# Pieces in neighbouring slots, one read per job, and half of the exponentials ahead of the carry copy

## The chip, the cores and the metric

The kernel runs on one core of one Trainium2 chip. The metric is the device time of one execution in microseconds; smaller is better. A core has five engines that each run their own instructions in order and wait for one another by semaphores: TensorE (PE in the profile, its weight loads PEld), VectorE (DVE), ScalarE (ACT), GpSimd (POOL) and SyncE (SP), which here issues the DMAs.

## The reference, cut to what matters

One block of a bidirectional selective state-space model for 16 sequences of 256 steps with 256 channels. Both directions run over all 16 sequences.

```
h, gate = adaln(x, c, ...)                    # normalise, scale, shift
def ssm(h, in_w, xproj_w, dt_bias, A_log, D, out_w):
    xs, z = split(h @ in_w)                   # 512 channels each
    xs = silu(xs)
    proj = xs @ xproj_w
    dt = softplus(proj[..., :512] + dt_bias)
    B, C = proj[..., 512:576], proj[..., 576:]
    A = -exp(A_log)                           # 512 channels x 64 states
    for t in steps:
        state = state * exp(dt_t * A) + (dt_t * xs_t) * B_t
        y_t = sum over states of state * C_t
    return (y + xs * D) * silu(z) @ out_w
x = x + gate * (ssm_forward(h) + flip(ssm_backward(flip(h))))
return x + gate2 * (silu(h2 @ w1) * (h2 @ w2) @ w3)
```

Before `proj`, the inputs of the two directions are prepared by matmuls. The sum over time with 512 x 64 states for each sequence and direction is the bulk of the work.

## The kernel before

There are two phases. `output_phase` does the last projections and is untouched. `main_phase` does all the rest in 16 **passes** (`PASSES`), one for each pair of sequences and direction. A pass has 128 **slots** (`JP`): eight chunks of 32 time steps, each with 16 slots. Slot j is one scan instruction of VectorE on 128 partitions (2 sequences x 64 states) by 1024 columns (32 channels x 32 steps), which holds two halves, h = 0 and 1, of 16 channels.

What a slot asks for, with the line numbers of the profile:

- **Inject** (TensorE, L1044, eight records a slot): spreads dt x xs x B into the PSUM tile `u`. `u` has two places, taken by j % 2, so the inject of slot j waits until scan j - 2 has ended.
- **Exponent** (TensorE, L1057, four records): for the slot j + 2, dt x A of half 0 and of half 1, each into one PSUM bank of 512 columns. They stand behind the inject of slot j. There are three banks (`NDT`, named `b_ex0` to `b_ex2`); `share_banks` hands them out in a fixed order, and what gets a bank waits until its last content has been read.
- **Decay** (ScalarE, `decay`, L802 and L803): for the slot j + 2, for each half, the exponential of the first column (`b_first`, only where there is a carry) and of the 31 others (`b_dA`). It frees the bank.
- **Carry** (GpSimd L578, L583, then ScalarE `put_carry`, L821): from the second chunk on, that is in slots 16 to 127, the state left by the chunk before is multiplied by the first decay, added to the first input, and copied by ScalarE over column 0 of `u`, once the inject of the same slot is there. The scan waits for it.
- **Scan** (VectorE, L894).
- **Readout** (TensorE, `add_up`, L1076): of the scans of eight slots before, in the odd slots, 16 records each; ScalarE reads the result every eighth slot (L814).

Beside this, in the slots of pass p the inputs of pass p + 1 are made in 31 **jobs**, laid into slots by the tables `XZ_SLOT`, `DT_SLOT`, `BC_SLOT`, `UT_SLOT`, `BT_SLOT`, `TURN_SLOT`. TensorE runs a piece of a job behind the slot's own work (`unit`): in an XZ job (L947) two matmuls of 128 x 256, in a DT or BC job (L955) four in two pieces, in a UT job or a turn job transposes. A job takes one of the three banks until ScalarE has read it: a DT job for three slots before the change. ScalarE's `unit` reads each job at the end of a slot (L658 and L661 for XZ, L677 and L678 for DT), works on it in SBUF (L665, L684 to L694), and changes its function table three times a pass (at L726, L741, L760). GpSimd multiplies and adds (L472 to L497). Passes 0, 2, ..., 12 also make the normalised input of the next pair of sequences: two turn jobs, of which each is read by ScalarE in two slots (`modulate`, L636). In the last pass there are no jobs.

ScalarE's order in slot j is: the carry copy of slot j, the decay of slot j + 2 (both halves), the read of the readout, the side work of `unit`. TensorE's order is: inject j, the exponents of j + 2, readout, job piece.

## Time and profile before

| what | us |
|---|---|
| median of 3 runs | 5272.7 (5270.68 to 5274.25) |
| the profiled execution | 5272.6 |
| its span, first to last instruction | 5270.9 |
| first scan starts, last scan ends (in the span) | 106.9, 4816.9 |
| VectorE busy in the span | 4721.3 |
| TensorE busy in the span | 4869.9 |
| ScalarE busy in the span | 3384.6 |
| idle time of VectorE ahead of a scan | 184.5 |

The profile is of one execution. Its times count from the first instruction. In a timeline each row is a run of like instructions that follow closely: its start, its length, engine, line, operation, output and inputs, their count, and in brackets the idle time of the engine before it with what ended it. The records of an engine overlap a little: a scan is recorded as 2.26 us long, and three that follow each other closely take less than three times that.

### The profile page before, as it was taken

Reading aid. Unit: us, or ns where it says so; the run is one execution under the profiler, and the core shown is the slowest. Engines: PE = TensorE matmul, PEld = TensorE weight load, DVE = VectorE, ACT = ScalarE, POOL = GpSimd, SP = SyncE. Lnnn points to the kernel's source line nnn. Section 1 sums busy time; section 2 is a strip of 40 time slices with the busy share of each in tenths; the row PEclk is TensorE's granted clock in tenths of the full one; section 3 lists DMA queues with packets and bytes.
Section 4 is the critical chain, followed back from the end, with each engine's and each line's share of the span. In section 5 each row is a group of like instructions: output and inputs, shape, how many; then the busy total and the mean of one; then the engine's idle time right before and its main releaser. Section 6 shows DMA issues by size and latency. Waiting matters only on the chain. (4 is left out here: it accounts for less than half of the span.)

```text
span 5270.9 us, 130492 instructions
## 1 busy us (share of the span) xinstructions
PE 4869.9 (92%) x44784; PEld 2658.3 (50%) x44784; DVE 4721.3 (90%) x2419; ACT 3384.6 (64%) x11498; POOL 3754.7 (71%) x6613
## 2 busy tenths in 40 slices
PE   6999999999999999999999999999999999776898
PEld 4555555555555555555555555555555555443444
DVE  2999999999999999999999999999999999996443
ACT  4767767676766766676766767676676767663112
POOL 4787878777787878777787878687887878674211
PEclk8999999999999999999999999999999999998999
DMA  3121211112121211112121211111121211113442
GB/s 107 39 65 45 65 38 54 56 39 62 43 61 44 66 41 50 56 40 62 43 61 43 67 40 52 55 45 56 43 61 43 64 40 46 31 29 111 145 153 68
DMA packets 433144, 306.75 MB, mean 58 GB/s; under 512 B 215920, under 2 KB 336240, under 8 KB 432496
## 3 DMA queue, kind: packets, MB, share of 16 engines
q1 hardware_dynamic: 428272, 294.39, 18.7%
q8 instruction: 349, 5.72, 0.4%
q10 hardware_dynamic: 4224, 4.19, 0.2%
q14 instruction: 299, 2.45, 0.1%
HBM read 187.27 MB, written 111.15 MB: 57 GB/s over the span
## 5 line engine op out<-in xcount | busy, mean ns | idle before, releaser
L894 DVE TENSOR_TENSOR_SCAN b_hs<-b_dA,b_u 128x1024 f32<-128x1024 f32 x2048 | 4536.0, 2270 | 184.5 <-ACT b_u L821 155.5
L1057 PE MATMUL b_ex<-b_dd,b_aw 32*128 32x512 f32 x8192 | 2751.5, 641 | 17.6 <-POOL b_dd L542 15.6
L1044 PE MATMUL b_u<-b_ud,b_bw 32*128 32x256 f32 x16384 | 2320.1, 400 | 276.9 <-DVE b_hs L894 255.9
L803 ACT ACTIVATE b_dA<-b_ex 128x496 f32<-128x496 f32 x4096 | 2303.5, 593 | 166.0 <-PE b_ex L1057 127.5
L1044 PEld LDWEIGHTS b_u<-b_ud,b_bw 32*128 32x128 f32 x16384 | 1417.5, 184 | 1122.7 <-issue 558.1
L821 ACT ACTIVATE b_u<-b_hin 128x32 f32<-128x32 f32 x1792 | 368.8, 206 | 1236.8 <-PE b_u L1044 1045.4
L542 POOL TENSOR_TENSOR b_dd<-b_dr,b_mask 128x512 f32<-128x512 f32 x1024 | 1074.9, 1050 | 51.5 <-DVE b_hs L894 39.8
L1076 PE MATMUL b_y<-b_hs,b_cw 128*32 128x256 f32 x16384 | 1104.8, 385 | 1.7 <-DVE b_hs L894 1.7
L551 POOL TENSOR_TENSOR b_ud<-b_ur,b_mask 128x512 f32<-128x512 f32 x1024 | 1085.6, 1060 | 0.0
L1057 PEld LDWEIGHTS b_ex<-b_dd,b_aw 32*128 32x128 f32 x8192 | 865.4, 183 | 62.0 <-ACT b_dA L803 35.7
L1076 PEld LDWEIGHTS b_y<-b_hs,b_cw 128*32 128x32 f32 x16384 | 426.9, 108 | 846.2 <-issue 663.3
L578 POOL TENSOR_TENSOR b_hm<-b_first,b_hs 128x32 f32<-128x32 f32 x1792 | 487.6, 272 | 443.5 <-ACT b_first L802 421.9
L802 ACT ACTIVATE b_first<-b_ex 128x16 f32<-128x16 f32 x3584 | 652.4, 182 | 56.4 <-PE b_ex L1057 33.2
L583 POOL TENSOR_TENSOR b_hin<-b_hm,b_u 128x32 f32<-128x32 f32 x1792 | 452.9, 253 | 140.4
L955 PE MATMUL b_ex<-b_xs,b_wxp 128*128 128x256 f32 x1256 | 353.4, 405 | 3.9 <-ACT b_ey L678 2.8
L1211 POOL TENSOR_TENSOR c_gs<-c_gs,c_sz 128x512 f32<-128x512 f32 x64 | 79.0, 1279 | 299.8 <-DVE c_gs L1417 299.8
L947 PE MATMUL b_ex<-b_hT,b_win 128*128 128x256 f32 x1004 | 285.9, 408 | 3.1 <-ACT b_hT L636 3.1
L955 PEld LDWEIGHTS b_ex<-b_xs,b_wxp 128*128 128x128 f32 x1256 | 214.5, 189 | 138.8 <-issue 118.6
L947 PEld LDWEIGHTS b_ex<-b_hT,b_win 128*128 128x128 f32 x1004 | 173.2, 191 | 117.5 <-issue 76.9
L477 POOL TENSOR_TENSOR b_ey<-b_wy,b_ey 128x512 f32<-128x512 f32 x64 | 83.4, 1304 | 202.5 <-ACT b_wy L694 202.5
L472 POOL TENSOR_TENSOR b_xs<-b_xs,b_th 128x512 f32<-128x512 f32 x64 | 81.4, 1273 | 193.2 <-ACT b_th L665 193.2
L472 POOL TENSOR_TENSOR b_sd<-b_sd,b_th 128x512 f32<-128x512 f32 x64 | 81.3, 1270 | 85.4 <-ACT b_th L665 85.4
(104 smaller groups left out, 2351.0 us busy)
## 6 DMA issues: line engine op xcount, KB each, us to landing
b_u<-scratch_ut SPq DMA_DIRECT2D x256, 128.0 KB, 2.9
scratch_y<-b_ysb SPq DMA_DIRECT2D x128, 256.0 KB, 2.1
scratch_xs<-b_xs SPq DMA_DIRECT2D x64, 256.0 KB, 2.5
scratch_sz<-b_sd SPq DMA_DIRECT2D x64, 256.0 KB, 2.2
scratch_dt<-b_sd SPq DMA_DIRECT2D x64, 256.0 KB, 2.1
scratch_ut<-b_uT SPq DMA_DIRECT2D x64, 256.0 KB, 2.6
b_ur<-scratch_ut SPq DMA_DIRECT2D x1024, 16.0 KB
b_dr<-scratch_dt SPq DMA_DIRECT2D x1024, 16.0 KB, 1.7
```

The lines of the kernel that those rows point to most:

```text
L542: nc.gpsimd.tensor_tensor(dd[:, (p * PAIRS + i) % NDD, :, :], dr[:, c % 2, v:v + 1, :].broadcast_to((P, TT, TC)), mask[:, :].unsqueeze(2). ...
L551: nc.gpsimd.tensor_tensor(ud[:, i % NPR, :, :, :], ur[:, c % 2, :, v * TT:(v + 1) * TT].unsqueeze(3).broadcast_to(shape), mask[:, :].unsqu ...
L578: nc.gpsimd.tensor_tensor(hm[:, j % NM, :, :].rearrange("p h d -> p (h d)"), e0[:, j % NM, :, :].rearrange("p h d -> p (h d)"), hs[:, v, : ...
L583: nc.gpsimd.tensor_tensor(hin[:, j % NM, :, :], hm[:, j % NM, :, :], u0[:, c % 2, 2 * kp:2 * kp + 2, v, :], ALU.add).then_inc(hin_made, 1)
L802: nc.scalar.activation(e0[:, j % NM, h, :], src[:, :, 0], ACT.Exp).then_inc(e0_done, 1)
L803: nc.scalar.activation(dA[:, j % NDA, h, :, 1:TC], src[:, :, 1:TC], ACT.Exp).then_inc(exp_done, 1)
L894: nc.vector.tensor_tensor_scan(hs[:, v, :, :, kp].rearrange("p d t -> p (d t)"), dA[:, j % NDA, :, :, :].rearrange("p h d t -> p (h d t)") ...
L947: last = nc.tensor.matmul(job_bank(n)[:, 0:SEQ], win[:, k, i * P:(i + 1) * P], hT[:, q % DIRS, k, b * SEQ:(b + 1) * SEQ], start=(k == 0), ...
L955: ins = nc.tensor.matmul(job_bank(n)[:, 0:SEQ], wxp[:, k, cols], xs[:, k, b * SEQ:(b + 1) * SEQ], start=(k == 0), stop=(k == JB - 1))
L1044: ins = nc.tensor.matmul(dst[:, :, tb, :], bw[row(r), c % 2, tb, :], ud[row(r), j // 2 % NPR, tb, :, :], start=(tb == 0), stop=(tb == NTB ...
L1057: nc.tensor.matmul(e[bank_of[what]][:, :], aw[row(r), p % DIRS, v, :, :].rearrange("p b s -> p (b s)"), dd[row(r), (p * PAIRS + j // 2) % ...
L1076: ins = nc.tensor.matmul(y[q * QR:(q + 1) * QR, cols], cw[:, n, q, g * QR:(g + 1) * QR], hs[:, f * (SPN // 2):(f + 1) * (SPN // 2), :, q * ...
```

## The change

Five things change in `main_phase`.

1. **ScalarE's slot.** `decay` is split by halves. The order in slot j is now: decay of slot j + 2, half 0; carry copy of slot j; a **read** of a job, if there is one; decay of slot j + 2, half 1; read of the readout; a step of the **work** on what was read. `unit` is split into two generators for it, `readers` and `works`.
2. **One read per job.** An XZ job is only copied out of its bank (`take_xz`); the tanh is then taken of both sequences at once from SBUF (`bend`, new). A DT job is read once with its bias into `pre`; Abs and Relu are taken later from SBUF at 512 columns. A semaphore `relued` is added, for which GpSimd's `sum_dt` waits, and `bent_up` ahead of `plus_one`.
3. **Slots.** The two pieces of a pair stand in neighbouring slots (0, 1), (4, 5) and so on, and the two pieces of a DT or BC job too, so that it holds its bank for two slots in place of three. All pieces now start at j % 4 = 0 or 1.
4. **Readouts** stand in the slots with j % 4 = 2 or 3, still two groups of eight records in each of four slots out of eight.
5. **Banks.** `share_banks` reckons with a bank of half 1 as free 0.5 slots after that of half 0 (0.25 before) and with one of a job 0.1 after its last slot. GpSimd's steps are moved by a few slots.

```diff
-        XZ_SLOT = ((0, 2), (4, 6), (8, 10), (12, 14), (16, 18), (86, 88), (98, 100), (104, 106))
-        DT_SLOT, DT_SPAN = (22, 38, 54, 70), 3
-        BC_SLOT, BC_SPAN = (32, 48), 3
-        UT_SLOT, UT_SPAN = (64, 80, 82, 96), (2, 2, 1, 1)
-        BT_SLOT = 66
+        XZ_SLOT = ((0, 1), (4, 5), (8, 9), (12, 13), (16, 17), (84, 85), (92, 93), (100, 101))
+        DT_SLOT, DT_SPAN = (20, 36, 52, 68), 2
+        BC_SLOT, BC_SPAN = (28, 44), 2
+        UT_SLOT = (60, 76, 80, 96)
+        BT_SLOT = 61
...
-                        give(("e", 2 * (slot + 2) + h), slot + 0.9 + 0.25 * h)
+                        give(("e", 2 * (slot + 2) + h), slot + 0.9 + 0.5 * h)
...
-                        give(("job", n), slot + slots + 0.2)
+                        give(("job", n), slot + slots + 0.1)
...
-                    nc.scalar.activation(dst[:, cols], job_bank(n)[:, 0:SEQ], ACT.Copy, scale=0.5)
-                    if m >= 2:
-                        act.wait_ge(silu_made, m - 1)
-                    nc.scalar.activation(th[:, i % 2, cols], job_bank(n)[:, 0:SEQ], ACT.Tanh, scale=0.5).then_inc(freed, 1)
+                    nc.scalar.activation(dst[:, b * SEQ:(b + 1) * SEQ], job_bank(n)[:, 0:SEQ], ACT.Copy, scale=0.5
+                                         ).then_inc(freed, 1)
+
+                def bend(q, i):
+                    m = q * SILUS + i
+                    src = xs[:, i, :] if i < JB else sd[:, i - JB, :]
+                    act.wait_ge(freed, first_job(q) + XZ_JOB[i] + CB)
+                    if m >= 2:
+                        act.wait_ge(silu_made, m - 1)
+                    nc.scalar.activation(th[:, i % 2, :], src, ACT.Tanh).then_inc(bent_up, 1)
...
-                    nc.scalar.activation(pre[:, m % 2, cols], job_bank(n)[:, 0:SEQ], ACT.Relu, bias=bias)
-                    nc.scalar.activation(ey[:, cols], job_bank(n)[:, 0:SEQ], ACT.Abs, bias=bias).then_inc(freed, 1)
+                    nc.scalar.activation(pre[:, m % 2, b * SEQ:(b + 1) * SEQ], job_bank(n)[:, 0:SEQ], ACT.Identity,
+                                         bias=dtb[:, q % DIRS, j:j + 1]).then_inc(freed, 1)
...
+                    nc.scalar.activation(ey[:, :], pre[:, m % 2, :], ACT.Abs).then_inc(bent, 1)
...
+                    nc.scalar.activation(pre[:, m % 2, :], pre[:, m % 2, :], ACT.Relu).then_inc(relued, 1)
...
+                        then = (p, j + 2) if j + 2 < JP else None if last else (p + 1, j + 2 - JP)
+                        if then:
+                            decay(*then, 0)
                         if j >= STEPS:
                             put_carry(p, j)
-                        if j + 2 < JP:
-                            decay(p, j + 2)
-                        elif not last:
-                            decay(p + 1, j + 2 - JP)
+                        next(reads, None)
+                        if then:
+                            decay(*then, 1)
                         if j % HALF == 0 and half >= 2:
                             read_y(half - 2)
-                        next(side, None)
+                        next(work, None)
...
-                    if k % 2 and half:
-                        add_up(half - 1, k % HALF - 1)
-                        add_up(half - 1, k % HALF)
+                    if k % 4 >= 2 and half:
+                        n = k % HALF // 4 * 2 + k % 4 - 2
+                        add_up(half - 1, 2 * n)
+                        add_up(half - 1, 2 * n + 1)
```

ScalarE before, slots 17 and 18 of the first pass (L821 is the carry copy, L802 and L803 the decay): the carry copy, then both halves, in each slot.

```order
L821 ACTIVATE b_u<-b_hin 128x32 [waits b_u_done3,b_u_done2,b_hin_made]
L802 ACTIVATE b_first<-b_ex2 128x16 [waits b_e_done0,b_hin_made,b_scanned]
L803 ACTIVATE b_dA<-b_ex2 128x16x31
L802 ACTIVATE b_first<-b_ex0 128x16 [waits b_e_done1]
L803 ACTIVATE b_dA<-b_ex0 128x16x31
L821 ACTIVATE b_u<-b_hin 128x32 [waits b_u_done1,b_u_done0,b_hin_made]
L802 ACTIVATE b_first<-b_ex1 128x16 [waits b_e_done2,b_hin_made,b_scanned]
L803 ACTIVATE b_dA<-b_ex1 128x16x31
L802 ACTIVATE b_first<-b_ex2 128x16 [waits b_e_done3]
L803 ACTIVATE b_dA<-b_ex2 128x16x31
```

The same engine after the change, slot 17 and the start of slot 18 (L835 and L836 are the decay, L854 the carry copy, L663 the read of an XZ job):

```order
L835 ACTIVATE b_first<-b_ex2 128x16 [waits b_e_done0,b_hin_made,b_scanned]
L836 ACTIVATE b_dA<-b_ex2 128x16x31
L854 ACTIVATE b_u<-b_hin 128x32 [waits b_u_done3,b_u_done2,b_hin_made]
L663 ACTIVATE b_sd<-b_ex0 128x256 [waits b_dt_stored0,b_full]
L835 ACTIVATE b_first<-b_ex1 128x16 [waits b_e_done1]
L836 ACTIVATE b_dA<-b_ex1 128x16x31
L835 ACTIVATE b_first<-b_ex2 128x16 [waits b_e_done2,b_hin_made,b_scanned]
L836 ACTIVATE b_dA<-b_ex2 128x16x31
L854 ACTIVATE b_u<-b_hin 128x32 [waits b_u_done1,b_u_done0,b_hin_made]
L835 ACTIVATE b_first<-b_ex0 128x16 [waits b_e_done3]
```

The carry copy moved behind the first half, and the read of the job stands between the carry copy and the second half.

TensorE before, slots 0 to 2 of the first pass, from the first job piece on (L947); `b_ex0` to `b_ex2` are the three banks:

```order
L947 MATMUL b_ex0<-b_hT,b_win 128x256 [waits b_exp_done,b_freed,b_win_loaded]
L947 MATMUL b_ex0<-b_hT,b_win 128x256
L1044 MATMUL b_u<-b_ud,b_bw 128x16x16 [waits b_scanned]
L1044 MATMUL b_u<-b_ud,b_bw 128x16x16 x3
L1057 MATMUL b_ex1<-b_dd,b_aw 128x512 [waits b_exp_done]
L1057 MATMUL b_ex2<-b_dd,b_aw 128x512 [waits b_exp_done]
L1044 MATMUL b_u<-b_ud,b_bw 128x16x16 [waits b_scanned,b_ud_made,b_dd_made]
L1044 MATMUL b_u<-b_ud,b_bw 128x16x16 x3
L1057 MATMUL b_ex0<-b_dd,b_aw 128x512 [waits b_freed]
L1057 MATMUL b_ex1<-b_dd,b_aw 128x512 [waits b_exp_done]
L947 MATMUL b_ex2<-b_hT,b_win 128x256 [waits b_exp_done]
```

TensorE after, the same place (L984 job piece, L1083 inject, L1096 exponent):

```order
L984 MATMUL b_ex0<-b_hT,b_win 128x256 [waits b_exp_done,b_freed,b_win_loaded]
L984 MATMUL b_ex0<-b_hT,b_win 128x256
L1083 MATMUL b_u<-b_ud,b_bw 128x16x16 [waits b_scanned]
L1083 MATMUL b_u<-b_ud,b_bw 128x16x16 x3
L1096 MATMUL b_ex1<-b_dd,b_aw 128x512 [waits b_exp_done]
L1096 MATMUL b_ex0<-b_dd,b_aw 128x512 [waits b_freed]
L984 MATMUL b_ex2<-b_hT,b_win 128x256 [waits b_exp_done]
L984 MATMUL b_ex2<-b_hT,b_win 128x256
L1083 MATMUL b_u<-b_ud,b_bw 128x16x16 [waits b_scanned,b_ud_made,b_dd_made]
L1083 MATMUL b_u<-b_ud,b_bw 128x16x16 x3
L1096 MATMUL b_ex1<-b_dd,b_aw 128x512 [waits b_exp_done]
L1096 MATMUL b_ex2<-b_dd,b_aw 128x512 [waits b_freed]
L1083 MATMUL b_u<-b_ud,b_bw 128x16x16 [waits b_scanned]
```

The piece of slot 2 moved to slot 1. An exponent that waits for the read of a job (`b_freed`) was that of half 0, two slots after the piece; it is now that of half 1, one slot after the piece.

ScalarE before, slot 113 of the first pass, where the second half of a turn job is read:

```order
L821 ACTIVATE b_u<-b_hin 128x32 [waits b_u_done3,b_u_done2,b_hin_made]
L802 ACTIVATE b_first<-b_ex2 128x16 [waits b_e_done0,b_hin_made,b_scanned]
L803 ACTIVATE b_dA<-b_ex2 128x16x31
L802 ACTIVATE b_first<-b_ex0 128x16 [waits b_e_done1]
L803 ACTIVATE b_dA<-b_ex0 128x16x31
L636 ACTIVATE b_hT<-b_ex1,mod 128x256 x2
```

and after:

```order
L835 ACTIVATE b_first<-b_ex2 128x16 [waits b_e_done0,b_hin_made,b_scanned]
L836 ACTIVATE b_dA<-b_ex2 128x16x31
L854 ACTIVATE b_u<-b_hin 128x32 [waits b_u_done3,b_u_done2,b_hin_made]
L643 ACTIVATE b_hT<-b_ex0,mod 128x256 x2
L835 ACTIVATE b_first<-b_ex0 128x16 [waits b_e_done1]
L836 ACTIVATE b_dA<-b_ex0 128x16x31
```

The reading of the turned input (two instructions, L636 before and L643 after) stood behind both halves of the decay; it now stands between them.

## Rows read from the trace of the kernel before

**Rows 1.** The page: busy time by engine; and the costliest group (columns: busy, mean ns | idle, releaser).

```profile
PE 4869.9 (92%) x44784; PEld 2658.3 (50%) x44784; DVE 4721.3 (90%) x2419; ACT 3384.6 (64%) x11498; POOL 3754.7 (71%) x6613
...
L894 DVE TENSOR_TENSOR_SCAN b_hs<-b_dA,b_u 128x1024 f32<-128x1024 f32 x2048 | 4536.0, 2270 | 184.5 <-ACT b_u L821 155.5
```

**Rows 2.** The scans (L894) in passes 2, 3 and 15: window, length, busy time, clock, DMA.

```profile
698.18:994.90 296.72, 284.17 (x130) 1.00 0.17 50
994.90:1289.18 294.28, 283.58 (x130) 1.00 0.18 53
...
4538.00:4816.90 278.90, 278.88 (x129) 0.99 0.09 25
```

**Rows 3.** The same of pass 3: slots 0-15, 20-35 and 84-103.

```profile
994.90:1030.98 36.08, 35.48 (x17) 1.00 0.17 49
...
1040.42:1078.30 37.88, 35.60 (x17) 1.00 0.16 47
...
1190.17:1235.66 45.49, 43.98 (x21) 1.00 0.29 86
```

**Rows 4.** Timeline (start, us, engine) of slots 40 to 42 of the last pass.

```profile
4622.97 6.62 DVE L894 TENSOR_TENSOR_SCAN b_hs<-b_dA,b_u 128x1024 f32<-128x1024 f32 x3
...
4623.20 0.48 PE L1044 MATMUL b_u<-b_ud,b_bw 32*128 32x256 f32 x2
...
4624.46 0.20 ACT L821 ACTIVATE b_u<-b_hin 128x32 f32<-128x32 f32 x1 [0.92 <-PE b_u L1044]
...
4625.28 0.48 PE L1044 MATMUL b_u<-b_ud,b_bw 32*128 32x256 f32 x2 [0.93 <-DVE b_hs L894]
...
4626.57 0.20 ACT L821 ACTIVATE b_u<-b_hin 128x32 f32<-128x32 f32 x1 [0.45 <-PE b_u L1044]
...
4627.56 0.48 PE L1044 MATMUL b_u<-b_ud,b_bw 32*128 32x256 f32 x2
```

**Rows 5.** Timeline of slot 14 of the last pass, where no carry is copied.

```profile
4566.58 0.48 PE L1044 MATMUL b_u<-b_ud,b_bw 32*128 32x256 f32 x2
...
4567.88 0.18 ACT L802 ACTIVATE b_first<-b_ex 128x16 f32<-128x16 f32 x1 [1.20 <-PE b_ex L1057]
...
4568.42 0.19 ACT L802 ACTIVATE b_first<-b_ex 128x16 f32<-128x16 f32 x1
```

**Rows 6.** Timeline of slots 18 and 19 of pass 2: a piece, then a readout.

```profile
737.37 0.48 PE L1044 MATMUL b_u<-b_ud,b_bw 32*128 32x256 f32 x2
...
738.45 1.13 PE L947 MATMUL b_ex<-b_hT,b_win 128*128 128x256 f32 x4
738.65 0.20 ACT L821 ACTIVATE b_u<-b_hin 128x32 f32<-128x32 f32 x1 [1.24 <-PE b_u L1044]
...
738.98 4.46 DVE L894 TENSOR_TENSOR_SCAN b_hs<-b_dA,b_u 128x1024 f32<-128x1024 f32 x2 [0.25 <-ACT b_u L821]
...
739.38 0.60 ACT L803 ACTIVATE b_dA<-b_ex 128x496 f32<-128x496 f32 x1
...
739.51 0.48 PE L1044 MATMUL b_u<-b_ud,b_bw 32*128 32x256 f32 x2
...
740.03 0.69 PE L1057 MATMUL b_ex<-b_dd,b_aw 32*128 32x512 f32 x1
...
742.09 0.48 PE L1044 MATMUL b_u<-b_ud,b_bw 32*128 32x256 f32 x2
```

**Rows 7.** Timeline of slot 6 of pass 2: a piece and its read.

```profile
711.17 1.13 PE L947 MATMUL b_ex<-b_hT,b_win 128*128 128x256 f32 x4
...
712.34 0.39 ACT L658 ACTIVATE b_xs<-b_ex 128x256 f32<-128x256 f32 x1
```

**Rows 8.** Timeline of slots 28 and 29 of pass 2: a table load and the scan behind.

```profile
763.78 1.28 ACT L741 ACT_TABLE_LOAD   x1
...
765.07 0.20 ACT L821 ACTIVATE b_u<-b_hin 128x32 f32<-128x32 f32 x1
```

**Rows 9.** Timeline of slot 113 of pass 2: the turned input is read.

```profile
960.94 1.11 ACT L636 ACTIVATE b_hT<-b_ex,mod 128x256 f32<-128x256 f32 x2
```

More of the change, by code:

```diff
@@ L178, in main_phase @@
         bent = sem("b_bent")
+        relued = sem("b_relued")
         logged = sem("b_logged")
@@ L765, in unit, with works @@
+                    if q % DIRS == 1 and q + 1 < PASSES:
+                        for k in range(MB):
+                            yield from modulate(q // DIRS + 1, k)
+                            yield from wait_steps(2)
+                def works(q):
+                    nc.scalar.preload_act_table_set("exp_and_others")
+                    yield from wait_steps(2)
+                    for i in range(JB + 1):
+                        bend(q, i)
                         yield
                         plus_one(q, i)
[L767 to L774 removed]
@@ L780, in _ @@
+                    nc.scalar.preload_act_table_set("exp_and_others")
+                    yield from wait_steps(4)
+                    for i in range(JB + 1, SILUS):
+                        bend(q, i)
+                        yield
+                        plus_one(q, i)
+                        yield from wait_steps(7)
                 act.wait_ge(made, 6)
@@ L786, in _ @@
                         pass
-                for _ in unit(0):
-                    pass
+                reads, work = readers(0), works(0)
+                for _ in range(JP):
+                    next(reads, None)
+                    next(work, None)
                 act.wait_ge(a_loaded, 16 * RT * DIRS * CB)
```

175 lines of the change are left out of this document (92 added, 83 removed).

## The prediction

> **What bounds the kernel now.** I read the busy times first. VectorE spends 4536.0 us of the 5270.9 us span in 2048 scans; its 184.5 us of idle time ahead of them is mostly (155.5 us) ended by ScalarE's carry copy [rows 1]. TensorE is busy about as long, so it is the second suspect. Then the passes: the last pass, which carries no jobs, takes 278.9 us, which is 128 scans at 2.178 us from start to start and no wait (three in 6.62 us, less 2.26 for the last [rows 4]); a pass with jobs takes 294.3 us, and 296.7 us where turn jobs are added [rows 2]. So jobs cost 15.4 and 17.8 us a pass, some 245 us in all, and that is the most that a better arrangement can bring. Inside a pass, 16 slots without a wait would take 34.85 us; rows 3 show 36.1 for slots 0 to 15, 37.9 for slots 20 to 35, and 45.5 where 20 slots need 43.6.
>
> Next, what a slot may take without holding the scan, from the job-free pass [rows 4]. Scans start at 4622.97, 4625.15 and 4627.33 and end 2.26 later. The inject starts 0.05 or 0.15 after the end of the scan that frees its place of u (4625.23 to 4625.28, 4627.41 to 4627.56). The carry copy starts 1.26 or 1.29 after the inject (4623.20 to 4624.46, 4625.28 to 4626.57). A scan that waits starts 0.33 after the start of the carry copy (738.65 to 738.98 [rows 6]). In rows 4 it starts 0.69 and 0.76 after it, so the slack is 0.36 us in the slot whose inject came 0.15 late and 0.43 in the other. The whole chain (scan ends, inject, carry, scan after next) has less than half a microsecond to spare even with no jobs.
>
> **Half of the decay ahead of the carry copy.** TensorE still runs inject, then exponents. The exponent of half 0 is ready for ScalarE no earlier than the inject is: where no carry stands before it and ScalarE idled for 1.20 us, its first exponential starts 1.30 after the inject (4566.58 to 4567.88), and the next half starts 0.54 later (4568.42) [rows 5]. So the carry copy can start 1.84 to 1.88 after the inject in place of 1.26 to 1.29, later by 0.58. Of that the slack covers 0.36 or 0.43. What is left, 0.22 or 0.15, sits in a loop that spans two scans, hence 0.11 or 0.075 a slot, 0.095 on average. A slot with a carry takes at least 2.178 + 0.095 = 2.27 us, four of them 9.1. This holds in all 112 carry slots of every pass. In the last pass nothing else changes: 112 x 0.095 = +10.6 us. What hides it where a job holds TensorE is nothing: there the inject itself is late.
>
> The Trainium skill (ScalarE: Activation LUTs, What ACT_TABLE_LOAD costs) gives an ACTIVATE with immediates 186 ns + 0.833 ns a column and lets neighbours overlap by about 93 ns. An estimate from that page is 0.61 us for a half (16 and 496 columns), not the 0.54 of rows 5; the floor would rise by a further 0.035 a slot, about 60 us over 1792 slots.
>
> **Pieces of jobs.** A piece in slot 18 starts 1.08 after the inject, and the next inject comes 2.14 after the last (737.37, 738.45, 739.51) [rows 6]. In the slot behind it, an exponent finds its bank still held: it starts 0.52 after the inject (740.03) in place of 0.03, since ScalarE's half 1 ran until 739.98 (739.38 + 0.60), and that slot takes 2.58 (to 742.09). A readout slot without such a hold takes 2.09. So before, a piece and the slot behind it take 4.72 us.
>
> After, that exponent waits for the read of the job. The read starts 0.04 after the piece ends (711.17 + 1.13 = 712.30 to 712.34) and takes 0.39 to 0.41 [rows 7]: inject + 1.08 + 1.13 + 0.04 + 0.40 = 2.65, and 0.05 to TensorE. The exponent then starts 2.70 - 2.14 = 0.56 after its inject, 0.53 late. Getting ScalarE out of the bank earlier by dropping the tanh brings nothing, as the read now stands between carry copy and half 1 and waits for the piece. With two pieces in neighbouring slots, two exponents are held: 2.14 + (2.14 + 0.53) + (2.09 + 0.53) + 2.09 = 9.5 us for four slots, against 2 x 4.72 = 9.44. DT pieces: half 1 holds the slot of the second piece by 0.54, the longer read (0.52) the next by 0.65, in all 9.65; BC 9.55. The number of holds is thus the same; they are only bunched.
>
> By stretch of slots, after: 0 to 15 have no carry and four XZ pairs, 3 x 9.5 and 9.8 for the first (a table load of 1.28 us [rows 8] stands behind slot 0's half 1, and delays the next slot's halves), 38.4 in all against 36.1 [rows 3], where half 1 ends earlier than in a carry slot and the hold was half as long. 16 to 19: 9.5. 20 to 51: two of 9.65 + 9.65 + 9.55 + 9.1 = 75.9. 52 to 83: two of 9.65 + 9.65 + 9.2 + 9.1 = 75.2. 84 to 103: three XZ pairs, one UT, one empty, 46.9 against 45.5 [rows 3]. 104 to 127: 6 x 9.1 = 54.6. The sum is 300.5 us.
>
> **Turn jobs.** The second half of a turned input is read behind the carry copy, for 1.11 us [rows 9], and the exponent of half 1 waits for it and the decay of half 1 for that. Inject + 1.33 + 0.55 + 0.14 + 1.11 + 0.05 = 3.18; its second record 0.53 later and 0.52 more to the next inject make a slot of 4.23 in place of 2.27. Twice a pass: +3.9, 304.4 us.
>
> **What is hidden or small.** Table loads: before, one stood behind two reads and the next carry copy had to follow it directly (763.78 + 1.28, then 765.07 [rows 8]); that wait of about a microsecond, and a like one later in the pass, go away, since in slots 22 and 82 the load now stands in a slot without a read. This is in the stretches above, as their sums have no term for it. Relu and Abs from SBUF cost ScalarE one more 512-column step a DT job; works stand behind half 1, where in rows 6 ScalarE waits for TensorE, and the read that they replace was as long. The wait on `relued` is met many slots ahead of `sum_dt`; behind it on GpSimd stand the next carries, which would be held if it were not. GpSimd (71% busy) gets the first decay of half 1 up to 0.6 us later in read slots, and has two slots before the carry is due. No DMA is added or resized. In the prologue the order of the same reads moves; I bound it by 3 us either way and take 0.
>
> The same page says that a table load costs 1.28 us and a drain of 1.38 more; rows 8 show the carry copy 0.01 us behind the load, so the trace doesn't bear the drain out. By the page, two loads a pass would hold a carry by about 1.5 us more each, some 45 us.
>
> **The sum.** Eight passes without turn jobs: 300.5 - 294.3 = +6.2 each, 50. Seven with: 304.4 - 296.7 = +7.7 each, 54. The last: +10.6. Together +114 us. The profiled execution took 5272.6 us (span 5270.9, 1.7 around it), 0.1 from the median of three runs, so the sum is 5387 us.
>
> **Rivals.** (a) The holds vanish. If the read freed the bank before the next exponent needs it (a piece that is ready sooner than rows 6 and 7 say), every group with pieces falls to 9.1, slots 0 to 15 stay at 36.1: 28 x 9.1 + 36.1 = 290.9 a pass, 3.4 less than now, with turn jobs 294.8, 1.9 less, and the last pass +10.6: 8 x 3.4 + 7 x 1.9 - 10.6 = 30 us faster, 5243. Against it speaks that TensorE must end the piece first. (b) The half is free. If the exponent of half 0 came ahead of the inject, or the carry copy were mostly late for GpSimd's sake, the half would run in idle time; up to the 155.5 us of waits go, and I price it at two thirds, 5170. Rows 5 speak against the first, and rows 4, where the carry copy is released by TensorE, against the second. (c) Worse than forecast: reads, a step of the logarithm and a late half 1 stack up in one ScalarE slot (slots 29, 45, 61), or GpSimd gets its first decay too late, and a carry is another microsecond late four times a pass: 15 x 4 = +60, 5447. (d) Nothing comes of it: gains and losses cancel within 10 us, as when the holds shrink by half. That the change doesn't do what it says is excluded by the order of the instructions.
>
> **How the numbers follow.** Forecast 0.70, (a) 0.08, (b) 0.06, (c) 0.12, (d) 0.04. A measurement can tell 0.2% (10 us) from no change. Faster is (a) and (b), 0.14; same is (d), 0.04; slower is the forecast and (c), 0.82. The range takes the forecast with the 0.05 or 0.15 of the inject (0.05 a slot in two scans, 0.025 x 1792 = 45 us), holds of 0.3 to 0.65, and (c): 5300 to 5470.
>
> **What would show it.** The scans of the last pass 2.27 us apart on average, from slot 16 on, and about 289 us for that pass. The carry copy 1.84 to 1.88 after the inject. In job slots, the exponent of half 1 about 0.56 after the inject, released by the read, in two slots of four. Slots 0 to 15 of a pass near 38.4. Idle time of VectorE behind the carry copy well above the 155.5 us of rows 1, and in most of the 1792 slots that have one. Waits for table loads gone. I am wrong if the last pass stays near 279 (rows 5 don't carry over), or if passes with jobs fall below 294.

## The result, and the profile after

The change makes the kernel slower by 5.9%: 5582.6 us (5579.09 to 5584.69) against 5272.1, ratio 1.0588 [1.057, 1.0606]. The forecast was 5387 us with a range of 5300 to 5470. The direction was right, the size was not: of the 310 us lost, 114 were foreseen. All times here and below are medians without two far slower executions, one of the kernel before (11121 us) and one of the kernel before with bunched readouts (8971 us).

Page of the changed kernel, in the columns of [rows 1]: VectorE's scans are L931 now, the carry copy L854, the first exponential L835, and L1096 is the exponent on TensorE.

```profile
PE 4847.9 (87%) x44784; PEld 2679.9 (48%) x44784; DVE 4802.2 (86%) x2419; ACT 3441.0 (62%) x11370; POOL 3757.5 (67%) x6613
...
L931 DVE TENSOR_TENSOR_SCAN b_hs<-b_dA,b_u 128x1024 f32<-128x1024 f32 x2048 | 4616.7, 2279 | 414.5 <-ACT b_u L854 325.4
...
L835 ACT ACTIVATE b_first<-b_ex 128x16 f32<-128x16 f32 x3584 | 664.3, 185 | 1364.9 <-PE b_ex L1096 1230.6
```

Two things stand out against [rows 1]. The idle time ahead of the scans went from 184.5 to 414.5 us, and the busy time of the scans grew too, by 81 us: the records of scans that follow closely overlap, those behind a wait do not (and are 2.29 us long, not 2.26). The scans and their idle time sum to 5031 us, 311 more than before, so the whole loss sits in the scan phase.

The cores view adds what no row of the page says loudly. Mean granted TensorE clock of the changed kernel, and of the kernel before:

```profile
core 0: 5580.1 us, clock 0.949
```

```profile
core 0: 5270.9 us, clock 0.989
```

The scans (L931) of the changed kernel in the last pass, in pass 5 (no turn jobs) and in pass 4 (turn jobs): window, length, busy time, clock, DMA. These answer to [rows 2].

```profile
4799.38:5124.38 325.00, 287.99 (x129) 0.86 0.08 22
1672.26:1979.48 307.22, 288.65 (x129) 0.98 0.17 50
1355.07:1672.26 317.19, 288.37 (x129) 0.96 0.16 47
```

The forecast had 289.5, 300.5 and 304.4 for them. The pass that carries no jobs, and should be the simplest to price, is the one that it missed by most, and it has the lowest clock. A mean of 0.86 over 325 us, with levels of 1 and one half, is 91 us at the lower level (1.2 GHz, the upper being 2.4), in 21 stretches. In the last pass of the kernel before it is 3 us. (These lengths, and those of low clock below, are counted in the trace's record of the granted clock; the rounded means of the rows give them within 3 us.)

Timeline of slots 44 to 46 of the last pass (ScalarE's carry copy, TensorE's inject L1083 and readout L1115, the scans):

```profile
4905.72 0.48 PE L1083 MATMUL b_u<-b_ud,b_bw 32*128 32x256 f32 x2 [0.36 <-DVE b_hs L931]
...
4907.56 0.21 ACT L854 ACTIVATE b_u<-b_hin 128x32 f32<-128x32 f32 x1
...
4907.81 0.48 PE L1083 MATMUL b_u<-b_ud,b_bw 32*128 32x256 f32 x2 [0.93 <-DVE b_hs L931]
...
4909.68 0.21 ACT L854 ACTIVATE b_u<-b_hin 128x32 f32<-128x32 f32 x1
...
4910.34 0.79 PE L1083 MATMUL b_u<-b_ud,b_bw 32*128 32x256 f32 x2 [1.37 <-DVE b_hs L931]
...
4912.37 1.73 PE L1115 MATMUL b_y<-b_hs,b_cw 128*32 128x256 f32 x16
...
4913.11 0.21 ACT L854 ACTIVATE b_u<-b_hin 128x32 f32<-128x32 f32 x1
...
4913.45 2.29 DVE L931 TENSOR_TENSOR_SCAN b_hs<-b_dA,b_u 128x1024 f32<-128x1024 f32 x1 [1.09 <-ACT b_u L854]
```

Slots 44 and 45 are as forecast: the carry copy starts 1.84 and 1.87 after its inject. These two slots hold neither piece nor readout. Behind them TensorE is at half speed: the first two records of the inject take 0.79 in place of 0.48, the carry copy of slot 46 starts 2.77 after its inject, and the scan idles 1.09. TensorE's row for slots 40 to 43 and for 44 and on (columns: us, PE busy, clock, DMA):

```profile
4896.49:4905.72 9.23, 6.57 (x80) 1.00 0.08 29
4905.72:4914.91 9.19, 6.89 (x64) 0.81 0.14 30
```

At full clock four slots without jobs take 9.23 us. The clock is down behind slots 45, 49, 53 and 57, and four slots then take 10.3 to 11.7; behind slots 37 and 41 it stays up. All 21 stretches of low clock in this pass begin at the end of the second of two such empty slots, or within 0.6 us behind it.

### The profile page after: what moved, and what is told of

Its sections match the earlier page's. It is cut to its first block and busy times, and to the rows that moved or that the text cites. A ratio compares the mean times of both kernels' runs of the same rounds, so it can differ in the third digit from the quotient of the medians.

```text
span 5580.1 us, 130554 instructions
## 1 busy us (share of the span) xinstructions
PE 4847.9 (87%) x44784; PEld 2679.9 (48%) x44784; DVE 4802.2 (86%) x2419; ACT 3441.0 (62%) x11370; POOL 3757.5 (67%) x6613
## 5 line engine op out<-in xcount | busy, mean ns | idle before, releaser
L931 DVE TENSOR_TENSOR_SCAN b_hs<-b_dA,b_u 128x1024 f32<-128x1024 f32 x2048 | 4616.7, 2279 | 414.5 <-ACT b_u L854 325.4
L1083 PE MATMUL b_u<-b_ud,b_bw 32*128 32x256 f32 x16384 | 2449.4, 414 | 584.1 <-DVE b_hs L931 542.1
L1096 PE MATMUL b_ex<-b_dd,b_aw 32*128 32x512 f32 x8192 | 2688.3, 669 | 44.2 <-ACT b_hT L643 27.8
L836 ACT ACTIVATE b_dA<-b_ex 128x496 f32<-128x496 f32 x4096 | 2399.2, 589 | 188.3 <-PE b_ex L1096 177.2
L1083 PEld LDWEIGHTS b_u<-b_ud,b_bw 32*128 32x128 f32 x16384 | 1503.5, 191 | 1481.9 <-issue 862.8
L835 ACT ACTIVATE b_first<-b_ex 128x16 f32<-128x16 f32 x3584 | 664.3, 185 | 1364.9 <-PE b_ex L1096 1230.6
L1115 PE MATMUL b_y<-b_hs,b_cw 128*32 128x256 f32 x16384 | 1185.2, 408 | 1.0 <-DVE b_hs L931 1.0
L1096 PEld LDWEIGHTS b_ex<-b_dd,b_aw 32*128 32x128 f32 x8192 | 798.1, 190 | 52.2 <-ACT b_hT L643 33.6
L1115 PEld LDWEIGHTS b_y<-b_hs,b_cw 128*32 128x32 f32 x16384 | 446.0, 113 | 734.7 <-issue 573.1
L854 ACT ACTIVATE b_u<-b_hin 128x32 f32<-128x32 f32 x1792 | 375.4, 209 | 5.5 <-PE b_u L1083 5.5
L984 PE MATMUL b_ex<-b_hT,b_win 128*128 128x256 f32 x1004 | 285.1, 408 | 3.1 <-ACT b_hT L643 3.1
L984 PEld LDWEIGHTS b_ex<-b_hT,b_win 128*128 128x128 f32 x1004 | 172.9, 191 | 143.2 <-ACT b_dA L836 77.9
L577 POOL TENSOR_TENSOR b_u<-b_u,b_b 128x256 f32<-128x256 f32 x224 | 137.4, 613 | 0.0
L847 ACT ACTIVATE b_ysb<-b_y 128x128 f32<-128x128 f32 x512 | 120.2, 306 | 8.0 <-PE b_y L1115 8.0
```

Of the source, the lines that this page charges most:

```text
L835: nc.scalar.activation(e0[:, j % NM, h, :], src[:, :, 0], ACT.Exp).then_inc(e0_done, 1)
L836: nc.scalar.activation(dA[:, j % NDA, h, :, 1:TC], src[:, :, 1:TC], ACT.Exp).then_inc(exp_done, 1)
L931: nc.vector.tensor_tensor_scan(hs[:, v, :, :, kp].rearrange("p d t -> p (d t)"), dA[:, j % NDA, :, :, :].rearrange("p h d t -> p (h d t)") ...
L984: last = nc.tensor.matmul(job_bank(n)[:, 0:SEQ], win[:, k, i * P:(i + 1) * P], hT[:, q % DIRS, k, b * SEQ:(b + 1) * SEQ], start=(k == 0), ...
L1083: ins = nc.tensor.matmul(dst[:, :, tb, :], bw[row(r), c % 2, tb, :], ud[row(r), j // 2 % NPR, tb, :, :], start=(tb == 0), stop=(tb == NTB ...
L1096: nc.tensor.matmul(e[bank_of[what]][:, :], aw[row(r), p % DIRS, v, :, :].rearrange("p b s -> p (b s)"), dd[row(r), (p * PAIRS + j // 2) % ...
```

## Experiments on ScalarE's order

The readouts stand in the odd slots here, as in the kernel before. All three runs are the kernel before with one or more exponentials moved ahead of the carry copy.

**One half ahead** (part 1 of the change alone):

```diff
+                        if then:
+                            decay(*then, 0)
                         if j >= STEPS:
                             put_carry(p, j)
-                        if j + 2 < JP:
-                            decay(p, j + 2)
...
+                        if then:
+                            decay(*then, 1)
```

> The kernel before with one thing of the change: half 0 of the decay stands ahead of the carry copy. Slots of jobs and readouts are those of before. Both theories: the carry copy 1.84 to 1.88 us after the inject in place of 1.26 to 1.29. Theory A: the clock falls as in the changed kernel, the last pass is 310 to 325 us, the whole 5380 to 5450. Theory B (the bunching makes the clock fall): the clock stays at 0.98, the last pass is 290 us (the floor of 2.27 us a slot), the whole 5320 to 5360.

Measured: 5408.6 us, ratio 1.026 [1.0242, 1.0279]. Its last pass:

```profile
4658.60:4952.08 293.48, 285.41 (x129) 1.00 0.09 24
```

The order alone costs 137 us, 49 us above the upper end of theory B, and the clock stays full in the last pass. So the moved half by itself does not make the clock fall there; over all passes it is low for 41 us, against 10 in the kernel before. The last pass lengthens by 14.6 us, not by 10.6. Passes with jobs take 301.1 to 304.0 us, with turn jobs 303.7 to 306.

**A small dose:** only the 16-column exponential (`b_first`) of half 0 goes ahead.

```diff
+                        if then:
+                            decay(*then, 0, rest=False)
                         if j >= STEPS:
                             put_carry(p, j)
...
+                        if then:
+                            decay(*then, 0, first=False)
+                            decay(*then, 1)
```

> The kernel before, but in each slot only the 16-column exponential of half 0 (b_first, recorded 0.18 us) stands ahead of the carry copy; its 31 columns and half 1 follow behind it. This is a small dose of the same delay. Theory (loop with slack): the carry copy starts about 1.41 after the inject in place of 1.26 to 1.29, less than the slack of 0.36 to 0.43, so the last pass stays at 278.9 us; only slots in which a scan already waits for the carry lose up to 0.12 us each. Total 5272 to 5310 us, clock as before. Rival (any ScalarE work ahead of the carry copy is paid in full, whatever its size): 0.12 to 0.15 us in half of 1792 slots or more, last pass about 287, total 5380 or more.

Measured: 5320.1 us, 1.0088 [1.0071, 1.0105]; the last pass:

```profile
4582.48:4861.61 279.13, 279.13 (x129) 1.00 0.09 25
```

The carry copy starts 1.40 to 1.44 after the inject, and the job-free loop swallows it, so the slack is there. The total is 10 us above what the theory of the loop gave: passes with jobs grow by 3.0 us each on average (1.9 to 4.4). Scans wait for the carry copy for 203.4 us in 485 waits here, against 155.5 in 415; that the scans which waited already pay the 0.12 to 0.15 us in full fits this, but was not shown one by one. The rival, that any work ahead of the copy is paid everywhere, falls by the last pass.

**A double dose:** both halves ahead of the carry copy.

```diff
+                        if then:
+                            decay(*then, 0)
+                            decay(*then, 1)
                         if j >= STEPS:
                             put_carry(p, j)
...
```

> The kernel before, but both halves of the decay stand ahead of the carry copy: double the dose of the run with one half ahead. Theory (loop over two scans): the carry copy starts about 2.52 after the inject, and two slots take 0.15 + 2.52 + 0.33 + 2.29 = 5.29 us, 2.645 each; the last pass takes 278.9 + 112 x 0.467 = 331 us, a pass with jobs 333 to 338, total 5800 to 5900 us. The clock stays near full, as readouts stand in every second slot as before. Rival (the clock falls because ScalarE's order leaves TensorE waiting): TensorE now idles for more than a microsecond in each slot, so the clock would fall in stretches without jobs, last pass 345 or more, total 6000 or more.

Measured: 5844.4 us, 1.1093 [1.1074, 1.1112]. Timeline in the last pass (L1049 is the inject, L823 the carry copy):

```profile
5143.07 0.48 PE L1049 MATMUL b_u<-b_ud,b_bw 32*128 32x256 f32 x2 [0.92 <-DVE b_hs L899]
...
5145.15 0.48 PE L1049 MATMUL b_u<-b_ud,b_bw 32*128 32x256 f32 x2 [0.93 <-DVE b_hs L899]
...
5145.44 0.24 ACT L823 ACTIVATE b_u<-b_hin 128x32 f32<-128x32 f32 x1
5145.80 4.46 DVE L899 TENSOR_TENSOR_SCAN b_hs<-b_dA,b_u 128x1024 f32<-128x1024 f32 x2 [0.71 <-ACT b_u L823]
...
5148.24 0.48 PE L1049 MATMUL b_u<-b_ud,b_bw 32*128 32x256 f32 x2 [0.92 <-DVE b_hs L899]
```

From inject to the inject after next it is 5.17 us. The carry copy stands 2.37 behind the inject (5143.07 to 5145.44), not 2.52 as I had it, and 2.40 in the other slot. The loop closes over the first of these slots: 2.37 to the carry copy, 0.36 more to the scan (5145.80), 2.29 for a scan behind a wait, 0.15 to the next inject but one, in all 5.17. My 5.29 had the same links with a carry copy too late by 0.15. Here the clock falls now and then too (0.95 in the last pass, 31 us), with no bunched readouts, which I had not expected; the slots are 2.585 us long by then, and TensorE is busy for 68% of the last pass.

## Experiments on the readouts and the clock

**Bunched readouts alone** (part 4 of the change, put into the kernel before):

```diff
-                    if k % 2 and half:
-                        add_up(half - 1, k % HALF - 1)
-                        add_up(half - 1, k % HALF)
+                    if k % 4 >= 2 and half:
+                        n = k % HALF // 4 * 2 + k % 4 - 2
+                        add_up(half - 1, 2 * n)
+                        add_up(half - 1, 2 * n + 1)
```

> The kernel before with one thing of the change: the readouts stand in the slots with j % 4 of 2 or 3 in place of the odd slots. Theory A: no effect on the clock or the last pass (279 us); passes with jobs within 2 us of before, since a piece and a readout meet in slot 2 of four and slot 1 is empty; the whole 5270 to 5300. Theory B: the clock falls in the last pass, which takes over 290 us, and the whole is over 5300.

Measured: 5494.8 us, 1.0423 [1.0401, 1.0446]; the last pass, in which ScalarE's order is that of before:

```profile
4750.03:5040.58 290.55, 280.94 (x129) 0.94 0.09 24
```

The part that I had not priced at all costs more alone (224 us) than the one on which the forecast rested (137). In the last pass, where it does nothing but move readouts of 16 matmuls from one slot to another, it costs 11.7 us, with 34 us of low clock. The length of a single gap does not decide this: no idle gap of TensorE in this last pass is longer than 1.11 us, while the run with the half ahead had gaps of up to 1.22 us in its last pass and kept the full clock.

**The changed kernel with the carry copy first again:**

```diff
-                        if then:
-                            decay(*then, 0)
                         if j >= STEPS:
                             put_carry(p, j)
+                        if then:
+                            decay(*then, 0)
```

> The changed kernel with one thing undone: in ScalarE's slot the carry copy stands first again, then half 0 of the decay, the read of a job, half 1. Theory A: the order on ScalarE makes the carry late, TensorE then waits for scans, and its granted clock falls to the lower level in short stretches; with the order undone both are gone. The last pass is 279 us (325.0 in the changed kernel), the mean clock 0.98 or more, passes with jobs 295 to 300, the whole 5290 to 5320. Theory B: the clock falls since the readouts and the pieces are bunched (slots 0 and 1 of four hold nothing where there is no job); then the clock stays near 0.95, the last pass above 295, the whole above 5380.

Measured: 5345.8 us, 1.0135 [1.0117, 1.0154]; the last pass:

```profile
4600.37:4893.82 293.45, 281.23 (x129) 0.92 0.08 24
```

Low clock with the order of before: 45 us of the last pass. With half 0 ahead as well it is 91. Neither theory had this: the low clock stays, as B says, but the total is 34 us below B's bound and 26 above A's. The two parts work on each other: the order leaves the clock alone when readouts are spread (1.00 above), but where two slots in a row are empty, it makes them longer and emptier.

**The changed kernel, kept busy:** two times four matmuls of zeros, added into the readout's sum, in slots 1, 4 and 5 of eight where no piece stands. The weights, `bt[:, 0, 0, 1, ...]`, are a block that is set to zero once and never written.

```diff
+                    for n in range(2):
+                        for q in range(QT):
+                            nc.tensor.matmul(y[q * QR:(q + 1) * QR, cols], bt[:, 0, 0, 1, 0:QR],
...
+                    if k % HALF in (1, 4, 5) and half and (last or j not in job_slots(p + 1)) and (last or j - 1 not in span_two):
+                        keep_busy(half)
```

> The changed kernel with work added: in the slots 1, 4 and 5 of eight that hold no piece, TensorE adds eight products with a block of zeros to the readout's bank (16 records, as a readout). Theory A and B: the clock falls for want of work on TensorE; with the filling the low stretches go from those places, the last pass falls from 325 to 288 to 295 us, passes without turn jobs from 307 to 302 to 304, the whole to 5420 to 5470, in spite of the added work. Theory C (the clock has nothing to do with TensorE's idle time): the last pass stays at 325 us or more and the whole at 5580 or more.

Measured: 5463.4 us, 1.0361 [1.0342, 1.0379]. Passes 4, 5 and 15:

```profile
1334.63:1647.47 312.84, 288.19 (x129) 0.98 0.16 48
1647.47:1949.61 302.14, 288.26 (x129) 1.00 0.18 51
4713.59:5007.08 293.49, 285.38 (x129) 1.00 0.09 24
```

More work for TensorE makes the kernel 119 us faster. Nothing else differs, and the low clock in the scan phase falls from 457 us to 73, so at least that much of the 310 us is clock. The last pass agrees to 0.01 us with that of the run that has only the half ahead (293.48).

The Trainium skill (TensorE: Matmul & The Clock Gate, The HAM clock gate) says that the clock has two levels and is set by how busy TensorE has been of late. The trace agrees with that: 0.86 in the last pass without the zeros, 1.00 with them.

**The changed kernel with the readouts in the odd slots again:**

```diff
-                    if k % 4 >= 2 and half:
-                        n = k % HALF // 4 * 2 + k % 4 - 2
-                        add_up(half - 1, 2 * n)
-                        add_up(half - 1, 2 * n + 1)
+                    if k % 2 and half:
+                        add_up(half - 1, k % HALF - 1)
+                        add_up(half - 1, k % HALF)
```

> The changed kernel with one part undone: the readouts stand in the odd slots again (k % 2), and nothing is added. Theory (the clock falls where two neighbouring slots hold neither a piece nor a readout): the last pass has a full clock and takes 293.5 us, the floor of the new ScalarE order alone, against 325.0 in the changed kernel; passes with jobs have hardly any low clock outside the turn slots, but a readout now shares a slot with the second piece of each pair, which costs about 10 us a pass: 312 without and 322 with turn jobs, total about 5500 us, clock above 0.98. Rival (the clock falls because of the order on ScalarE together with the jobs' new places): low clock for over 200 us, last pass above 300.

Measured: 5661.4 us, 1.0739 [1.0723, 1.0756], 160 us more than expected. Pass 5 and the last pass:

```profile
1713.72:2029.52 315.80, 285.77 (x130) 1.00 0.17 49
4914.08:5207.56 293.48, 285.38 (x129) 1.00 0.08 24
```

On the clock the theory held: full in both, and 293.48 again. On the jobs it did not: 315.8, where 312 was expected, and 325.3 to 326.5 with turn jobs (322 expected). Slots 4 to 7 of pass 5 show a part of it:

```profile
1725.31 1.08 PE L1115 MATMUL b_y<-b_hs,b_cw 128*32 128x256 f32 x16
1726.32 1.13 PE L984 MATMUL b_ex<-b_hT,b_win 128*128 128x256 f32 x4
...
1727.48 0.38 ACT L663 ACTIVATE b_xs<-b_ex 128x256 f32<-128x256 f32 x1 [1.87 <-PE b_ex L984]
```

The second piece of a pair now stands behind the readout, the read waits for the piece (ScalarE idles 1.87), and half 1 of the decay stands behind the read. My total of about 5500 did not even fit my own passes: 8 x 312 + 7 x 322 + 293.5, with 104 us ahead of the first scan and 456 behind the last, are 5604. The miss that is left is 4 us a pass.

## Experiments at full clock

**Carry copy first, and kept busy.** The changed kernel with both edits shown above; what is left of the change is neighbouring pieces, one read per job and bunched readouts.

> The changed kernel with the carry copy first again (ScalarE's order of before within the slot), and with added matmuls of zeros in slots 1, 4 and 5 of eight where no job piece stands. What is left of the change is: neighbouring pieces, one read per job, readouts in slots 2 and 3 of four. Theory (all that the version without the added matmuls lost was clock): clock above 0.985, last pass 279 us, passes without turn jobs 293 to 296, with turn jobs 297 to 303, total 5265 to 5320 us against 5346 without the added matmuls. Rival (bunched work costs as much by holding banks and late injects): the clock is full but the passes stay at 297 to 300 and the total near 5345.

Measured: 5313.3 us, 1.0082 [1.0065, 1.0099]. Passes 8 (turn jobs), 9 and 15, then slots 112 to 127 of pass 8:

```profile
2494.14:2797.42 303.28, 283.90 (x130) 0.99 0.17 49
2797.42:3090.89 293.47, 283.17 (x129) 1.00 0.18 53
4579.79:4858.64 278.85, 278.85 (x129) 1.00 0.09 26
2753.98:2797.42 43.44, 35.17 (x18) 0.92 0.08 23
```

Against the kept-busy kernel with half 0 ahead, all 150 us are the order: 14.6 in the last pass and 9 on average in each of the others (8.7 in pass 9 against pass 5 above). Passes without turn jobs are as long as before the change (293.5 against 294.3 of [rows 2]). So the new places and the single reads, taken together and at full clock, neither bring nor cost anything there, as the count of holds in the forecast said; what each does alone was not measured. All that is left over is in the turn slots: 43.4 us, where slots 112 to 127 take 34.8 without turn jobs.

**The kernel before with bunched readouts, kept busy** by the same matmuls, in slots 1, 4 and 5 of eight where no piece of that kernel stands.

> The kernel before with the readouts in slots 2 and 3 of four, and the same added matmuls of zeros in slots 1, 4 and 5 of eight where no job piece stands. The version without them took 5498 us. Theory (part clock, part a readout that now shares a slot with a job piece, which makes that slot longer than a scan): clock above 0.985, last pass 279 us, passes with jobs 300 to 304, total 5380 to 5430 us. Rival (it was all clock): passes with jobs at 294 to 297, total 5280 to 5300.

Measured: 5429.0 us, 1.03 [1.0283, 1.0317]. Passes 9 and 15:

```profile
2860.63:3165.20 304.57, 283.33 (x129) 1.00 0.17 51
4693.69:4972.53 278.84, 278.84 (x129) 1.00 0.09 26
```

The clock was 66 us of what bunching cost the kernel before (5494.8 to 5429.0). The rest, 10 us in each pass with jobs, is a readout that shares a slot with a piece, since the pieces stood in even slots there: slots 6, 10 and 14 of pass 9, which hold both, take 3.15 us by the starts of their scans, where the kernel before has 2.20. With the pieces in slots 0 and 1 and the clock kept up (the run of 5313 us), a pass without turn jobs is as long as before, bunched readouts and all.

**The bank of the turn jobs:** one number in the planner, in the run of 5313 us.

```diff
-                        give(("job", n), slot + slots + 0.1)
+                        give(("job", n), slot + slots + (0.45 if j in TURN_SLOT else 0.1))
```

> The version with the carry copy first and the added matmuls of zeros (5313 us), with one number changed: the planner of banks takes a turn job as held 0.45 slots after its last slot, not 0.1. So the bank of a turn job goes to the exponent of half 0 two slots later, as in the kernel before, and no longer to that of half 1 one slot later. Theory (the 44.8 us of the turn slots, against 34.8 without turn jobs, come from TensorE waiting for the second read of the turned input and from the clock that falls behind that wait): slots 112 to 127 take 36.5 to 39 us with turn jobs, no low clock there, a pass with turn jobs 296 to 298 in place of 303.6, total about 5270 us. Rival (it is the 1.11 us of reading between carry copy and half 1): slots 112 to 127 stay above 42 us, total above 5300.

Measured: 5265.8 us (5262.07 to 5269.02), 0.9993 [0.9984, 1.0002], no difference from the kernel before that can be told. Pass 8, and its slots 112 to 127:

```profile
2464.63:2761.37 296.74, 283.81 (x130) 1.00 0.17 50
2724.40:2761.37 36.97, 35.06 (x18) 1.00 0.10 27
```

That the bank went to the exponent of half 1, which then waited for the turned input, cost 47 us in seven passes, part of it through the clock (0.92 in the row above, 1.00 here).

**The read behind half 1:** the same run of 5313 us with two edits.

```diff
-                        next(reads, None)
                         if then:
                             decay(*then, 1)
+                        next(reads, None)
...
-                        give(("job", n), slot + slots + 0.1)
+                        give(("job", n), slot + slots + 0.45)
```

> The same version (carry copy first, added matmuls of zeros, 5313 us) with two edits: the read of a job stands behind half 1 of the decay, and the planner of banks takes every job as held 0.45 slots after its last slot, so that its bank goes to an exponent two slots later. Theory (what neighbouring pieces and one read per job still cost is the exponent of half 1 that waits for the read): slots 0 to 15 back from 38.0 to about 36 us, the turn slots near 37, passes 291 to 294 without and 293 to 297 with turn jobs, total 5235 to 5270 us, at or below the kernel before. Rival (the read behind half 1 holds the next piece or the next half as long as before): passes stay at 293.5 and the total at 5270 or above.

Measured: **5134.8 us** (5132.02 to 5136.78), 0.9742 [0.9729, 0.9755]: 2.6% faster than the kernel before, and 100 us better than the lower end of what was expected. Its scans on the page, then passes 8, 9 and 15, and slots 0 to 15 of pass 9:

```profile
L931 DVE TENSOR_TENSOR_SCAN b_hs<-b_dA,b_u 128x1024 f32<-128x1024 f32 x2048 | 4505.2, 2267 | 81.2 <-ACT b_u L854 40.8
```

```profile
2397.07:2685.16 288.09, 282.31 (x129) 1.00 0.18 52
2685.16:2969.27 284.11, 281.16 (x129) 1.00 0.19 55
4399.47:4678.31 278.84, 278.84 (x129) 1.00 0.09 26
...
2685.16:2720.52 35.36, 35.14 (x18) 1.00 0.18 50
```

Slots 0 to 15 take 35.36 us, the time of 16 scans at 2.178 within 0.5 us, with eight pieces beside them (36.1 before, [rows 3]). The carry copy has fallen from 155.5 to 40.8 us of idle time. Half 1 does not wait for a piece any more, and the bank of a piece goes to an exponent that comes two slots later. I had expected to win back only the one hold that these edits remove. A hold also makes the next inject late, and with it the next carry, which may be the rest; no run parts the two edits, so what each brings is open.

**The same without the zeros:**

> The fastest version so far (carry copy first, read behind half 1, bank of a job given on two slots later, added matmuls of zeros; 5134.8 us) without the matmuls of zeros. Theory (with the readouts in slots 2 and 3 of four, TensorE's clock falls where slots 0, 1, 4 and 5 of eight hold no work): the last pass goes from 278.8 back to about 293 us with some 45 us of low clock, as in the version with the carry copy first and nothing added (293.45), passes with jobs 285 to 292, total 5170 to 5220 us, mean clock 0.96 to 0.98. Rival (the low clock came from TensorE waiting for the reads of the jobs, which this order has ended): clock above 0.985 and 5135 us, so that the added matmuls were never needed.

Measured: 5210.4 us, 0.9885 [0.9869, 0.9902]. The last pass:

```profile
4459.18:4751.54 292.36, 281.07 (x129) 0.93 0.09 24
```

The theory holds for the clock: 13.5 us in the last pass, with 42 us of low clock, and 76 us in all hang on the added matmuls, even when no job makes TensorE wait. Three of the passes with turn jobs come out longer than expected, up to 296.6 us where 292 was the bound. Without the zeros the version is still 1.1% faster than before.

## Why the prediction missed

- **Half of the decay ahead of the carry copy.** Right in mechanism and nearly in size. The carry copy starts 1.84 and 1.87 after the inject, and the last pass at full clock has a floor above that of before. The step "What is left, 0.22 or 0.15, sits in a loop that spans two scans, hence 0.11 or 0.075 a slot, 0.095 on average" is off: the scans of both parities run on one engine, so the slower of the two chains counts for both: 0.15 + 1.84 + 0.33 + 2.29 = 4.61, seen as 4.62 for two slots (4905.72 to 4910.34), 2.31 each and not 2.27. Measured: +14.6 us in the last pass against +10.6. The scan's 2.29 behind a wait, not 2.26, is part of it.
- **"In the last pass nothing else changes".** This is the step that failed. The readouts move there too (part 4 of the change), and the forecast has no term for them, in that pass or any. They leave two slots in a row with 1.2 us of work for TensorE in each (slots 44 and 45 above), and the clock drops behind such pairs, 21 times in the last pass, at 1.5 us a drop. Measured: 325.0 against 293.49 kept busy, 31.5 us in the last pass, 119 us in the whole.
- **Pieces.** Right at full clock. The hold is where it was said, 0.55 after the inject (second record of slot 5, pass 5, at 1682.26 + 0.55):

```profile
1682.26 0.48 PE L1083 MATMUL b_u<-b_ud,b_bw 32*128 32x256 f32 x2
...
1682.37 0.38 ACT L663 ACTIVATE b_xs<-b_ex 128x256 f32<-128x256 f32 x1 [0.36 <-PE b_ex L984]
...
1682.81 0.69 PE L1096 MATMUL b_ex<-b_dd,b_aw 32*128 32x512 f32 x2
```

  The stretches of pass 5, slots 0 to 15, 20 to 35 and 84 to 103, answer to [rows 3] and to forecasts of 38.4, 38.0 and 46.9; the fourth row is slots 112 to 127 of pass 4, the turn slots:

```profile
1672.26:1710.81 38.55, 35.69 (x18) 1.00 0.15 46
1720.42:1758.33 37.91, 36.20 (x18) 1.00 0.14 41
1873.12:1920.29 47.17, 45.18 (x21) 1.00 0.34 104
1626.30:1672.26 45.96, 36.09 (x17) 0.85 0.08 22
```

- **Turn jobs.** The first half was right: the exponent of half 1 starts 3.07 after the inject, where 3.18 was foreseen. What follows was not. In slot 113 of pass 2 (L643 reads the turned input):

```profile
1001.97 1.02 ACT L643 ACTIVATE b_hT<-b_ex,mod 128x256 f32<-128x256 f32 x2
1003.04 1.22 PE L1096 MATMUL b_ex<-b_dd,b_aw 32*128 32x512 f32 x1 [1.92 <-ACT b_hT L643]
```

  TensorE idles 1.92 us, and the exponent's record is 1.22 long where it was 0.69. The clock fell during the wait, and the exponents of the next slot are slow and late in their turn. Slots 112 to 127 took 46.0 us against the 40.3 foreseen (four groups of 9.1, and 3.9), and in the kept-busy run they still take 46.4 in pass 4, with 10 us of low clock, which is 9.8 more than without turn jobs (36.6 in pass 5), against the 3.9 foreseen.
- **The sum of the miss.** In the profiled execution the passes are 197 us longer than forecast. The kept-busy run splits it: 118 us lie between it and the changed kernel (32 in the last pass, 52 in the eight passes without and 34 in the seven with turn jobs), and are the clock's; 41 are the turn term (7 x 5.9); 35 and 4 are what the passes with jobs (15 x 2.3) and the last are longer than forecast at full clock. In the last pass that is the floor. It would give 4 us in each of the others too, so some term there came out shorter than forecast; which one is open.
- **Idle time in most of 1792 slots.** Wrong: VectorE waits for the carry copy 574 times, 415 before. In the job-free loop only every second scan waits, for 0.15 (4903.29 and 4907.90 follow such waits), and the one behind it follows directly.

```profile
DVE b_hs L931 <- ACT b_u L854: 325.4, 574, 3.8
```

- **Table loads.** Half right. The load of slot 22 delays nothing: in pass 5 the carry copy of slot 23 starts 1.87 after its inject, as in any other slot. The one of slot 82 still does: in the kept-busy run, at full clock, the carry copy of slot 83 of pass 5 starts 2.39 after its inject, about 0.5 late.
- **The rivals.** (a) is excluded by slots 0 to 15 of pass 5, 38.55 us and not 36.1; (b) by the run with the half ahead. (c), a stack-up on ScalarE, would have given 5447, but is not seen: the carry copies of slots 29, 45 and 61 of pass 5 start 1.87 after their injects. The list had no rival on another engine's clock. My range was laid around the terms that I had, not around the parts of the change.

Left open: how much of the turn term is the clock and how much the waiting itself. The turn slots keep a clock of 0.92 in the run of 5313 us, and one edit mended both.

## What to carry to other kernels

Price every part of a change, also the one that only moves work about on an engine that is not the bound: put TensorE's work into a table by slot, and where a change leaves neighbouring slots nearly empty, as here, look at the granted clock first in the profile after. In a loop with slack, add up the whole chain over all its scans and take the slowest, not the average of what each exceeds by. And let the read of side work stand behind what the main loop waits for, giving its bank to the consumer that comes latest: here the two together, the turn jobs' 47 us among it, were worth 178 us at full clock.

## What the runs showed of the hardware

- TensorE's clock went to its lower level (1.2 GHz) 21 times in a last pass in which no idle gap of TensorE was longer than 1.5 us; what preceded it each time was two slots with inject and exponents alone. With the bunched readouts alone it did so with no gap above 1.11 us, and with the half ahead alone it did not, with gaps of up to 1.22. At the lower level an inject's first records take 0.79 us, not 0.48, a readout 1.73 us, not 1.08.
- Matmuls of zeros into a sum that is being made keep the clock up, and the kernel gains 119 us (with half 0 ahead) or 76 us (read last) by work that it doesn't need.
- A scan that starts after a wait is recorded as 2.29 us, one that follows another directly as 2.26.
- Where both halves of the decay follow each other directly, the second starts 0.54 us after the first ([rows 5]; 0.54 and 0.55 with both halves ahead); with the carry copy between them, 0.66 after it (4907.02 to 4907.68 in the changed kernel).
